# First guess of a sparsemax threshold: from mean and variance instead of one measured step, and a closing measure split two and two

## The reference, cut to what matters

```
x = x + tanh(g_xattn[0]) * attention(layernorm(x), ctx, ctx, Wq, bq, Wk, bk, Wv, bv, Wo, bo)
x = x + tanh(g_ffn[0]) * moe(layernorm(x), router_w, w_in, b_in, w_out, b_out)

# in attention, per batch and head
scores = q_h @ k_h.T * 16 ** -0.5                # 512 x 1601
zs = sort(scores, descending); cssv = cumsum(zs) - 1
k = number of positions r with zs[r] > cssv[r] / r
tau = cssv[k] / k
attn = clip(scores - tau, 0)                     # rows sum to 1
out = attn @ v_h
```

## Time and profile before

| | us |
|---|---|
| median of 3 runs | 6868.18 (6863.97 to 6875.29) |
| profiled execution | 6908.67, its span 6906.8 |
| VectorE busy over the span | 6013.8 (87%) |
| ScalarE busy | 5556.3 (80%) |
| TensorE busy | 5085.9 (74%), mean granted clock 0.73 |
| GpSimd busy | 2471.6 (36%) |

### The profile page before, as it was taken

One profiled execution on the slowest core, in us unless ns is written; L12 is line 12 of the kernel. 1 busy time (PEld: TensorE's weight loads), 2 busy tenths in 40 slices (PEclk: granted clock), 3 DMA queues, 4 the chain that ended last, 5 costly groups with the idle time before them and its releaser, 6 DMA issues. The chain is left out here.

```text
span 6906.8 us, 164803 instructions
## 1 busy us (share of the span) xinstructions
PE 5085.9 (74%) x19554; PEld 1673.0 (24%) x19555; DVE 6013.8 (87%) x50066; ACT 5556.3 (80%) x12484; POOL 2471.6 (36%) x10299
## 2 busy tenths in 40 slices
PE   8895777776777677676777777777777777767695
PEld 5551111111111111111111111111111111136574
DVE  4558999999999999999999999999999999957445
ACT  3336998998999999898999999999999999942221
POOL 2222333333333333333333333333333333324432
PEclk9995676676667766666766676666666676677798
DMA  5762111111111111111111111111111111145235
GB/s 194 238 201 56 30 34 29 31 35 28 31 31 32 31 31 31 30 30 29 28 31 32 31 32 31 33 29 31 31 35 32 32 32 33 28 152 207 89 100 204
DMA packets 691615, 415.98 MB, mean 60 GB/s; under 512 B 503712, under 2 KB 597536, under 8 KB 690208
## 3 DMA queue, kind: packets, MB, share of 16 engines
q1 hardware_dynamic: 677408, 370.58, 21.4%
q0 software_dynamic: 13056, 35.74, 1.4%
HBM read 249.13 MB, written 156.88 MB: 59 GB/s over the span
## 5 line engine op out<-in xcount | busy, mean ns | idle before, releaser
L887 DVE MAX8 a_cand<-a_scores 128x8 f32<-128x42 f32 (+1 forms) x38912 | 4395.9, 199 | 176.8 <-issue 140.9
L633 ACT ACTIVATE a_junk_act<-a_cand,a_ntau 128x304 f32<-128x304 f32 (+1 forms) x3840 | 1933.4, 522 | 145.2 <-POOL a_ntau L964 49.7
L603 PE MATMUL a_ring<-a_q,a_k 99*128 99x512 bf16 (+1 forms) x3328 | 1472.0, 556 | 764.1 <-ACT a_scores L669 499.3
L548 PE MATMUL a_out<-a_attn,a_v 128*32 128x512 f32 (+1 forms) x6656 | 1418.0, 793 | 518.8 <-ACT a_attn L673 518.8
L669 ACT COPY a_scores<-a_ring 128x1024 f32<-128x1024 f32 (+1 forms) x2048 | 1611.3, 830 | 154.0 <-PE a_ring L599 83.5
L673 ACT ACTIVATE a_attn<-a_ring 128x1024 f32<-128x1024 f32 (+1 forms) x1792 | 1654.1, 975 | 52.1 <-PE a_ring L603 50.9
L599 PE MATMUL a_ring<-a_k,a_q 96*128 96x512 bf16 (+1 forms) x4096 | 1336.5, 454 | 75.9 <-DVE a_ident L700 33.7
L633 ACT ACTIVATION_READ_ACCUMULATOR a_junk_act<-a_cand,a_ntau 128x1 f32 x3840 | 798.5, 208 | 0.0
L599 PEld LDWEIGHTS a_ring<-a_k,a_q 96*128 96x128 bf16 x4096 | 385.9, 116 | 1427.6 <-ACT a_attn L673 646.2
L603 PEld LDWEIGHTS a_ring<-a_q,a_k 99*128 99x128 bf16 (+1 forms) x3328 | 286.9, 118 | 1603.2 <-ACT a_scores L669 877.5
L548 PEld LDWEIGHTS a_out<-a_attn,a_v 128*32 128x32 f32 (+1 forms) x6656 | 174.4, 122 | 1189.0 <-ACT a_attn L673 718.9
(11 more groups left out here) (232 smaller groups left out, 6369.2 us busy)
## 6 DMA issues: line engine op xcount, KB each, us to landing
a_k<-k_parts SPq DMA_DIRECT2D x1536, 50.0 KB
k_parts<-p_ks SPq DMA_DIRECT2D x48, 800.5 KB, 7.3
o_parts<-a_o SPq DMA_DIRECT2D x512, 64.0 KB, 1.6
e_o<-o_parts SPq DMA_DIRECT2D x64, 512.0 KB
p_ctx<-in_ctx_t SPq DMA_DIRECT2D x16, 1601.0 KB, 8.6
v_heads<-p_v SPq DMA_DIRECT2D x16, 1536.0 KB
a_q<-q_parts SPq DMA_DIRECT2D x1536, 16.0 KB
a_v<-v_heads SPq DMA_DIRECT2D x256, 96.0 KB
```

The lines of the kernel that those rows point to most:

```text
L548: mm = nc.tensor.matmul(out_ps[at:at + 2 * HEAD_DIM], beside, attn[0:rows, k, (c % 2) * BANK:(c % 2 + 1) * BANK], start=first and c < 4, s ...
L603: mm = nc.tensor.matmul(at[0:rows, m * BANK:(m + 1) * BANK], k_st[0:SCORE_ROWS + TAU_ROWS, ut, c * P:c * P + rows], q_st[0:SCORE_ROWS + TA ...
L633: ins = nc.scalar.activation(into[:, t].rearrange("p (a b) -> p a b", b=CHUNKS), cand[:, u % SLOTS, t, 0:w], ACT.Relu, bias=ntau[:, u % 2, ...
L887: ins = V.max(cand[:, u % SLOTS, t, :, c], scores[:, u % SLOTS, t, lo:hi])
```

## The change

`start` makes the largest and the eighth largest as before, then runs a batch-norm statistic (`bn_stats`) per tile over the 76 values of the two highest ranks. Its six outputs per row are count, mean and summed squared deviation of one half of the values, and the same of the other half. VectorE adds the two sums (`spread_sq`); GpSimd, first thing in its step, makes the guess from them in six instructions (`guess`): tau = mean - 0.01207 + 15.41 v - 303.7 v², with v the sum over 76, at most 0.02. The measured first step and the seven small instructions around it leave VectorE. The count moves to t = 1. In t = 0 `start` now comes before the closing measure, and the closing measure covers two tiles on VectorE and two on ScalarE (ACT_LAST, 3 before). BEFORE_LAST rises from 3e-4 to 5e-4. The wait of VectorE for `tau_split` goes.

```diff
-USUAL_COUNT = 22.0
+GUESS_AT, GUESS_SPREAD, GUESS_BEND, MOST_SPREAD = -0.01207, 15.41, -303.7, 0.02
 ROUNDS = 4
 EXACT = 3e-5
-BEFORE_LAST = 3e-4
+BEFORE_LAST = 5e-4
-ACT_LAST = 3
+ACT_LAST = 2
...
             def start(i, u, link):
-                c, nt = cand[:, u % SLOTS], ntau[:, u % 2]
-                if not isinstance(i, int) or i >= 2:
-                    dve.wait_ge(tau_split, i - 1)
-                    dve.sem_inc(passed, 1)
+                c, st = cand[:, u % SLOTS], stats[:, u % 2]
                 V.tensor_reduce(tops[:, u % 2].rearrange("p r t -> p t r"), c[:, :, 0:8:7], AX.X, ALU.max, negate=True)
-                yield from link(V.tensor_reduce(w1[:], c[:, :, 0], AX.X, ALU.add))
-                yield from link(V.tensor_scalar(nt, w1[:], -1.0 / CHUNKS, None, ALU.mult))
-                for t in range(TILES):
-                    ins = measure_own(t, c[:, t, 0:FIRST], CHUNKS * FIRST, nt)
-                yield from link(ins)
-                e = own_excess[:]
-                V.scalar_tensor_tensor(out=w2[:], in0=e, scalar=1.0, in1=e, op0=ALU.subtract, op1=ALU.mult)
-                yield from link(V.tensor_scalar(w1[:], e, 1.0, None, ALU.add))
-                yield from link(V.reciprocal(w1[:], w1[:]))
-                yield from link(V.scalar_tensor_tensor(out=w3[:], in0=w2[:], scalar=-2.0 / USUAL_COUNT, in1=w1[:], op0=ALU.mult, op1=ALU.mult))
-                V.tensor_tensor(nt, nt, w3[:], ALU.add).then_inc(guessed, 1)
-                yield
+                for t in range(TILES):
+                    ins = V.bn_stats(st[:, t], c[:, t, 0:FIRST].rearrange("p a b -> p (a b)"))
+                yield from link(ins)
+                V.tensor_tensor(spread_sq[:, u % 2], st[:, :, 2], st[:, :, 5], ALU.add).then_inc(spread_made, 1)
+                yield
+
+            def count(i, u, link):
+                c, nt = cand[:, u % SLOTS], ntau[:, u % 2]
                 dve.wait_ge(guessed, i + 1)
                 for t in range(TILES):
                     ins = measure_count(t, c[:, t, 0:SECOND], CHUNKS * SECOND, nt, count4[:, t:t + 1])
...
+                    if t == 0 and has(i, 1):
+                        dve.wait_ge(cand_made, i)
+                        yield from start(i - 1, prev, link)
                     if t == 0 and has(i, 2):
                         for _ in range(3):
                             yield
...
-                    if t == 0 and has(i, 1):
-                        dve.wait_ge(cand_made, i)
-                        yield from start(i - 1, prev, link)
+                    if t == 1 and has(i, 1):
+                        yield from count(i - 1, prev, link)
...
+                def guess(i, u):
+                    st, nt = stats[:, u % 2], ntau[:, u % 2]
+                    pool.wait_ge(spread_made, i + 1)
+                    pool.sem_inc(passed_pool, 1)
+                    G.tensor_tensor(center[:], st[:, :, 1], st[:, :, 4], ALU.add)
+                    link(G.tensor_scalar(vary[:], spread_sq[:, u % 2], 1.0 / (FIRST * CHUNKS), MOST_SPREAD, ALU.mult, ALU.min))
+                    G.tensor_scalar(center[:], center[:], -0.5, -GUESS_AT, ALU.mult, ALU.add)
+                    link(G.tensor_scalar(near[:], vary[:], -GUESS_BEND, -GUESS_SPREAD, ALU.mult, ALU.add))
+                    link(G.tensor_tensor(near[:], near[:], vary[:], ALU.mult))
+                    G.tensor_tensor(nt, center[:], near[:], ALU.add).then_inc(guessed, 1)
...
+                if has(i, 1):
+                    guess(i - 1, (u - 1) % U)
                 if has(i, 2):
                     last_step(i - 2, (u - 2) % U)
```

More of the change, by code:

```diff
@@ L437, in attend_program @@
         excess = sb("excess", [P, 2, ROUNDS, TILES])
-        own_excess = sb("own_excess", [P, TILES])
+        stats = sb("stats", [P, 2, TILES, 6])
+        spread_sq = sb("spread_sq", [P, 2, TILES])
+        center, vary, near = (sb(n, [P, TILES]) for n in ("center", "vary", "near"))
         count4 = sb("count4", [P, TILES])
         per_count = sb("per_count", [P, 2, TILES])
-        w1, w2, w3 = (sb(n, [P, TILES]) for n in ("w1", "w2", "w3"))
+        w1 = sb("w1", [P, TILES])
         over, bend, newton, depth = (sb(n, [P, TILES]) for n in ("over", "bend", "newton", "depth"))
@@ L473, in attend_program @@
         counted = sem("counted")
+        spread_made = sem("spread_made")
         tau_tried = sem("tau_tried")
@@ L716, in zeros_like @@
                 return (zeros[:].unsqueeze(2) if len(values.shape) == 3 else zeros[:]).broadcast_to(list(values.shape))
-            def measure_own(t, values, width, nt):
-                return V.scalar_tensor_tensor(out=view(junk, values, width, TILES + t), in0=values, scalar=nt[:, t:t + 1], in1=zeros_like(values), op0=ALU.add, op1=ALU.max,
-                                              accum_out=own_excess[:, t:t + 1])
             def measure_count(t, values, width, nt, into):
@@ L731, in start @@
             def start(i, u, link):
-                c, nt = cand[:, u % SLOTS], ntau[:, u % 2]
-                if not isinstance(i, int) or i >= 2:
-                    dve.wait_ge(tau_split, i - 1)
-                    dve.sem_inc(passed, 1)
-                V.tensor_reduce(tops[:, u % 2].rearrange("p r t -> p t r"), c[:, :, 0:8:7], AX.X, ALU.max, negate=True)
-                yield from link(V.tensor_reduce(w1[:], c[:, :, 0], AX.X, ALU.add))
-                yield from link(V.tensor_scalar(nt, w1[:], -1.0 / CHUNKS, None, ALU.mult))
-                for t in range(TILES):
-                    ins = measure_own(t, c[:, t, 0:FIRST], CHUNKS * FIRST, nt)
-                yield from link(ins)
-                e = own_excess[:]
-                V.scalar_tensor_tensor(out=w2[:], in0=e, scalar=1.0, in1=e, op0=ALU.subtract, op1=ALU.mult)
-                yield from link(V.tensor_scalar(w1[:], e, 1.0, None, ALU.add))
-                yield from link(V.reciprocal(w1[:], w1[:]))
-                yield from link(V.scalar_tensor_tensor(out=w3[:], in0=w2[:], scalar=-2.0 / USUAL_COUNT, in1=w1[:], op0=ALU.mult, op1=ALU.mult))
-                V.tensor_tensor(nt, nt, w3[:], ALU.add).then_inc(guessed, 1)
-                yield
+                c, st = cand[:, u % SLOTS], stats[:, u % 2]
+                V.tensor_reduce(tops[:, u % 2].rearrange("p r t -> p t r"), c[:, :, 0:8:7], AX.X, ALU.max, negate=True)
+                for t in range(TILES):
[4 more added lines that the diff above has]
+            def count(i, u, link):
+                c, nt = cand[:, u % SLOTS], ntau[:, u % 2]
                 dve.wait_ge(guessed, i + 1)
@@ L762, in slope @@
                 V.reciprocal(per_fall[:], w1[:]).then_inc(inv_made, 1)
-            FIRST_LINKS, LAST_LINKS = 2 + 1 + 3 + 2 + 1, 2
+            FIRST_LINKS, LAST_LINKS = 1 + 2 + 1, 2
             def links_before(i):
@@ L900, in _ @@
             G = nc.gpsimd
-            FIRST_LINKS, LAST_LINKS = 6 + 4 + 5, 5 + 3
+            FIRST_LINKS, LAST_LINKS = 3 + 6 + 4 + 5, 5 + 3
             def links_before(i):
```

## The result

The changed kernel takes 9807.43 us (median of 4 runs, 9801.37 to 9808.68) against 6867.3 us before: ratio 1.4277, 95% interval 1.4252 to 1.4302. The forecast was 9804 us. The profiled execution has a span of 9804.7 us.

A forecast was written before the change was run, and what follows sets the result against it. VectorE was taken to end the attention stage's items: 3841 + 1317 us for items, 1771 for tiles, 1518 for steps make 8447 against 5511 us, +2936. Added to 6868 that forecast 9804 us, range 9600 to 10080.

The forecast's parts named there:

- The number of settled tiles: Attention stage, all 256 items: 325 tiles in 193 items bad and 186 steps needed, by the kernel's formulas in float32.
- even and odd places make the halves: In the statistic over 76 values: each half mixes both ranks, so the fitted constants don't suit and the guess is too high.
- Rivals 2 and 3: Statistic's halves of one rank: the second with the wait, 7090 us, chance 0.06; the third without it, 6816 us, 0.05.
- rival 2: Statistic's halves of one rank, with the wait before L752: 54 tiles, 11 steps, +222, 7090 us; chance 0.06.
- The price of a tile and a step: Settling on VectorE: 5.45 us per settled tile and 8.16 us per step, 1771 and 1518 us in all.
- The wait in front of L752: VectorE, t = 3: waits 1.34 us in items without settling, making them 21.24 us; settled tiles hide it.
- The chain: Count, GpSimd's `second`, ScalarE's round 1, `third`, round 2 and `fall`, ending in front of VectorE's slope: needs 10.47 us.
- VectorE's own way between the two: VectorE from count to slope: 82 MAX8 instead of 98, 1.76 us less, leaving 9.13 us.
- VectorE's own length: VectorE's time per item without waits or settling: 0.32 us less than 20.22, so 19.90 us (19.7 to 20.1).
- four statistics: VectorE's added instructions of 76 columns in `start`: 0.64 us for four per item, bounds 0.44 to 0.86.
- the list without MAX8: VectorE's instructions per item: 1.47 us removed, 0.06, 0.45 and 0.64 added, net 0.32 us less.
- Rival 1: Settled tiles hold GpSimd instructions that VectorE later waits for: 325 x 1.67 = +543, 10340 us; chance 0.07.

The follow-up runs named there:

- the reordered statistic: Changed kernel with its own constants, the statistic reading the 76 values chunk by chunk (largest, second largest, largest, ...): 7103.52 us in a single run.

## Why the prediction was right

- *The number of settled tiles* decided it, and it came from arithmetic: 325 tiles and 186 steps forecast, 319 and 186 run. That even and odd places make the halves was taken, with no row for it; the reordered statistic showed it. Rivals 2 and 3 fell with that; rival 2's price, 7090 us, is what the reordered kernel took (7104).
- *The price of a tile and a step*: 5.45 and 8.16 forecast, 5.30 and 8.10 by the fit. 45 of the earlier trace rows were enough to price 505, since a settled tile is the same closed piece of VectorE's queue each time.
- *The wait in front of L752*: 1.34 us forecast, 1.00 measured, absent in items with settling as forecast. The chain was as long as read in the earlier trace rows: from L747 to L752 are 1103.44 - 1092.96 = 10.48 us, and 10.47 was forecast. It was VectorE's own way between the two that was under-priced: 9.13 us forecast, 10.48 - 0.81 = 9.67 here. Of the 0.54 us, 0.35 is the idle time behind the loop, 0.75 us in this step where it was 0.40 in the item of the earlier trace rows. Another 0.11 is that the 16 MAX8 taken away were priced at 0.11 us each, where 50 in a row take 3040.62 - 3035.45 = 5.17 us, 0.103 each. The rest is the overlap of L752 with the last MAX8, which is lost when L752 waits. The lines of the kernel before:

```profile
3035.45 5.28 DVE L887 MAX8 a_cand<-a_scores 128x8 f32<-128x42 f32 x50
3040.62 0.13 DVE L816 SCALAR_TENSOR_TENSOR a_tile_bits<-a_turn,a_weigh 1x4 f32<-1x4 f32 x1
...
3042.10 4.26 DVE L887 MAX8 a_cand<-a_scores 128x8 f32<-128x42 f32 x40 [0.40 <-issue]
```

- *VectorE's own length* was the term that was mis-sized: 19.90 us forecast, 20.43 by the fit for items with settling beside their tiles and steps. The instructions came out better than forecast, since four statistics take 1086.33 - 1085.77 = 0.56 us and not 0.64, and the list without MAX8 is 0.41 us shorter, not 0.32. But a shorter list did not shorten the item: the same fit over the kernel before gives 20.38 us for this term, not the 20.22 of one undisturbed item from which 19.90 was taken. In items with settling VectorE's idle time between the settling and its next MAX8 is 1.50 us on average, 1.27 before, and 0.15 us of waits for ScalarE's copies stand in them, none before. In items without settling, passing the loop takes 0.57 us on average in the new program instead of 0.40, and none of the kernels got such an item below 20.26 us in the median. That the sum came out within 3 us is luck, because errors offset each other: 191 x 0.53 us = +101 for this term, -9 tiles in the intervals and 0.15 us less for each, together -96.
- *Rival 1*, settled tiles that hold GpSimd, is there and costs nothing that shows: a tile takes 5.30 us by the fit, less than the 5.45 forecast. In the item with the tile above, GpSimd over time:

```profile
1119.88 1.68 POOL L965 TENSOR_SCALAR a_over<-a_excess 128x4 f32<-128x4 f32 x1 [1.77 <-ACT a_junk_act L636]
1121.76 0.19 POOL L966 TENSOR_SCALAR a_bend<-a_over 128x4 f32<-128x4 f32 x1 [0.19 <-POOL a_over L965]
```

L965 takes 1.68 us beside L774, where it takes 0.24 alone. VectorE reached L752 seven us later and did not wait. Over the run L965 has a median of 1620 ns (238 before for the same line), so most settled items have such a hold, and none shows in front of L752. The Trainium skill, SBUF — State Buffer, "SBUF: two separate sides", has this as an exclusive lock between a VectorE instruction with two SBUF inputs and a GpSimd instruction that reads SBUF, for the whole instruction. By that rule the trace agrees: L965 begins 0.30 us after L774 and ends 0.09 us after it.

What stays open: why an item without settling stays at 20.5 to 20.65 us on average when L752 is hardly waited for. 0.17 us of it is the dearer passing of the loop. The traces show small waits at five places of the ring (VectorE for ScalarE's copies, ScalarE for GpSimd's tau of rounds 1, 2 and 3 and for TensorE's scores); no experiment here shortened the ring itself, for instance with the guess on VectorE.

## What to carry to other kernels

When a fast path guards itself with a test and a slow path, count how often the slow path runs before pricing anything else, with the kernel's own arithmetic on the real inputs; the count of the kernel before tells whether that arithmetic can be trusted. Constants fitted to a statistic belong to the exact set of values that the instruction puts in it: fit them on what the instruction reads, in its order. And an instruction moved within a queue in order is priced twice: once for itself and once for the distance to the next wait of the chain that begins with it.

## What the runs showed of the hardware

- The batch-norm statistic puts the elements at even places of its stream in one triple and those at odd places in the other, in both shapes tried: read as 76 in a row it gave 319 settled tiles (325 by this split, 54 by halves of the first and last 38), read as 38 x 2 it gave the 54 (65 - 11) that the alternating split predicts. Over 76 columns it takes 224 ns, 0.14 us from start to start.
- Reading a word and passing an empty loop cost VectorE 0.39 to 0.42 us at some places of its program and 0.72 to 0.77 us at others, the same in each turn of the unrolled steps, and two instructions more in each step, which no one waits for, moved seven of the twelve places from the first to the second. Why, no view shows.
- The entry of a second or later tile took longer in most items of the changed kernel: of its 126 such entries 38 wait 1.62 us in the median, as the earlier trace rows have it, and 88 wait 1.94 us with a cause called remote, 172.9 us in all, against 1.9 us in the kernel before. What they wait for no view shows.
- VectorE's full measure (1887 ns) made a GpSimd instruction of 0.24 us last until its own end (1.68 us), and no wait of VectorE for GpSimd's `fall` came of it.
